# Fused cross-attention and mixture-of-experts kernel: every engine's calls in the attention loop put in another order

## The reference

```python
x = x + xattn(layernorm(x), c, c, Wq, bq, Wk, bk, Wv, bv, Wo, bo, alpha)
x = x + ffn(layernorm(x), Wr, W1, b1, W2, b2)
# xattn, per block of 128 tokens: 16 heads of 16; scores = alpha * 4 * (q.k) / (|q| + |k|)**2 ; softmax over the 128 keys ; @ v ; @ Wo + bo
# ffn: logits = x @ Wr, softmax, top 2 of 8 experts, weights normalised ;
#      out = sum over the 2 experts of weight * (gelu(x @ W1[e] + b1[e]) @ W2[e] + b2[e]),  W1 256 x 1024, W2 1024 x 256
```

## Time and profile before

| | before |
|---|---|
| median of 3 runs | 882.54 us |
| the profiled execution, its own time | 875.53 us |
| its span, first to last instruction | 872.7 us |
| mean granted TensorE clock | 0.985 |
| TensorE busy | 815.5 us (93%) |
| VectorE, ScalarE, GpSimd busy | 644.1, 585.9, 481.2 us |
| the attention loop, first `factors(0)` to the last one's pass | 34 to 458 us |
| the 71 slots | from about 458 us on |

### The profile page before, as it was taken

How to read it: one execution, slowest core, us unless ns; L and a number is a source line. 1 busy time by engine, 2 the same in 40 slices (tenths; PEclk the granted TensorE clock), 3 DMA queues, 4 the chain that set the end, 5 groups by cost and what they waited for, 6 DMA issues and landing times. The chain is left out here.

```text
span 872.7 us, 28779 instructions
## 1 busy us (share of the span) xinstructions
PE 815.5 (93%) x9479; PEld 697.5 (80%) x9479; DVE 644.1 (74%) x2593; ACT 585.9 (67%) x1206; POOL 481.2 (55%) x604
## 2 busy tenths in 40 slices
PE   3899999999999999999888999999999999999995
PEld 2667777777767777777667999999999999999984
DVE  6558688988888888889877788666666666666554
ACT  1488988889888889888866655555555555555542
POOL 5347676879878799887766235422222222222322
PEclk9799999999999999999989999999999999999998
DMA  4212332233322445432459845433333233333221
GB/s 144 81 33 74 98 98 76 83 112 99 123 88 82 162 142 177 135 118 94 148 171 333 280 72 113 97 50 52 50 49 51 50 52 51 51 52 51 39 29 22
DMA packets 61887, 84.69 MB, mean 97 GB/s; under 512 B 9872, under 2 KB 55312, under 8 KB 59568
## 3 DMA queue, kind: packets, MB, share of 16 engines
q1 hardware_dynamic: 47504, 64.26, 23.1%
q0 software_dynamic: 13296, 18.00, 12.3%
q10 hardware_dynamic: 944, 0.60, 0.2%
HBM read 49.86 MB, written 31.92 MB: 94 GB/s over the span
## 5 line engine op out<-in xcount | busy, mean ns | idle before, releaser
L1721 POOL DMA_INDIRECT out<-yw,rb x71 | 111.3, 1567 | 259.0 <-DVE yw L1498 228.1
L1627 POOL TENSOR_TENSOR tw<-tw,tm 128x512 f32<-128x512 f32 x128 | 161.9, 1279 | 43.7 <-DVE tm L1207 43.3
L997 ACT ACTIVATE h<-s_ps,b1t,inv 128x128 f32<-128x128 f32 x288 | 105.0, 467 | 91.3 <-PE s_ps L746 91.2
L997 ACT ACTIVATE h<-u_ps,b1t,inv 128x128 f32<-128x128 f32 x280 | 102.2, 467 | 91.1 <-PE u_ps L746 91.1
L1477 DVE TENSOR_SCALAR hs<-h,hsc 128x512 f16<-128x512 f32 (+1 forms) x146 | 71.0, 486 | 105.7 <-ACT h L997 102.6
L1207 DVE CUSTOM_DVE_ANT_0 tw<-th,s_ps 128x128 f32<-128x128 f32 x512 | 111.7, 282 | 39.1 <-PE s_ps L546 19.0
L1479 DVE SCALAR_TENSOR_TENSOR hs<-h,hsc,hs 128x512 f16<-128x512 f32 (+1 forms) x146 | 107.7, 738 | 5.2
L746 PE MATMUL s_ps<-xt,w1s 128*128 128x128 f16 x1728 | 102.9, 219 | 0.5 <-DVE xt L1464 0.5
L746 PE MATMUL u_ps<-xt,w1s 128*128 128x128 f16 x1680 | 101.8, 221 | 1.1 <-DVE xt L1464 0.6
L770 PE MATMUL pv_ps<-w2s_sb,hs 128*128 x864 | 100.7, 273 | 0.1
L746 PEld LDWEIGHTS s_ps<-xt,w1s 128*128 x1728 | 98.2, 98 | 0.9 <-DVE xt L1464 0.8
(11 more groups left out here) (261 smaller groups left out, 1456.9 us busy)
## 6 DMA issues: line engine op xcount, KB each, us to landing
wl<-L_ffn_W SPq DMA_DIRECT2D x16, 1024.0 KB, 5.3
rb<-xrec SPq DMA_DIRECT2D x71, 132.5 KB, 2.1
w2s<-wst SPq DMA_DIRECT2D x8, 1024.0 KB, 4.6
w2s_sb<-w2s SPq DMA_DIRECT2D x8, 1024.0 KB, 7.3
xin<-x SPq DMA_DIRECT2D x32, 128.0 KB
cin<-ctx SPq DMA_DIRECT2D x32, 128.0 KB, 3.4
xres<-x SPq DMA_DIRECT2D x32, 128.0 KB, 2.3
out<-x SPq DMA_DIRECT2D x30, 128.0 KB, 1.7
```

What stands on the lines that cost most here:

```text
L997: ins = act.activation(h32[n % HBANKS][:, m % width, :], hbank[n % HBANKS][:, o:o + SLOT], ACT.Gelu, scale=inv1[:, bass.ds(ex, 1)].bitcast ...
L1627: pool.tensor_tensor(tw[h][:, i, :, :], tw[h][:, i, :, :], tm[h][:, 4 * i:4 * i + 4].unsqueeze(2).to_broadcast([P, 4, P]), ALU.subtract).t ...
L1721: pool.indirect_dma_start(out[:, :], bass.IndirectOffsetOnAxis(ap=rb[j][:, D + NE:D + NE + 1], axis=0), yw[s % 2][:, :], None, compute_op= ...
```

## The change

No instruction is added or taken out. All five engines' calls in the loop stand in another order, and many with another pair offset, so that a "pass" of the code begins at another place; the banks of the turns are dealt out anew (`TURNS`). SyncE's `store_pads` goes from its end to its front. In the last pair's turns `oc1` gets bank 2 and `wo1` bank 0; VectorE's `residual(0, NP - 1)` goes ahead of `hidden_scales`; ScalarE's `weight_high(NP - 1)` goes into the last pass, ahead of `record_high(0)`. The calls themselves are not edited. In the diff below the indentation is cut by 12, and for TensorE, ScalarE and GpSimd, and the first half of VectorE's, only the new order is shown (the old one stands in the kernel above); "..." marks where old lines are left out.

```diff
@@ -61,18 +61,18 @@
 TURNS = [
-    ("oc0", -5, "ote", 0, 2), ("ex30", -5, "ex30", None, 1), ("rank", -7, "rpos", None, 0), ("ex31", -5, "ex31", None, 2),
-    ("kv1", -3, "qke1", None, 1), ("q1", -3, "qke1", None, 0), ("kv0", -3, "qke0", None, 2), ("q0", -3, "qke0", None, 1),
-    ("ex00", -4, "ex00", None, 1), ("ob1", -5, "on", 1, 2), ("wo0", -5, "x10", None, 0), ("oc1", -5, "ote", 1, 2),
-    ("ex01", -4, "ex01", None, 2), ("ex10", -4, "ex10", None, 1), ("wgr", -4, "wdg", None, 0), ("qk_t0", -3, "kte0", None, 2),
-    ("wo1", -5, "x11", None, 1), ("qk_t1", -3, "kte1", None, 0), ("ex11", -4, "ex11", None, 2), ("rows_t", -3, "rowq", None, 1),
-    ("xct1", -2, "xce1", None, 2), ("xct0", -2, "xce0", None, 0), ("ex20", -4, "ex20", None, 1), ("ex21", -4, "ex21", None, 0),
-    ("ob0", -4, "on", 0, 2), ("wsum", -4, "wcl", None, 1),
+    ("xct0", -3, "xce0", None, 1), ("qk_t0", -4, "kte0", None, 2), ("wo1", -6, "x11", None, 0), ("ex11", -5, "ex11", None, 2),
+    ("qk_t1", -4, "kte1", None, 1), ("rows_t", -4, "rowq", None, 0), ("ex20", -5, "ex20", None, 2), ("wsum", -5, "wcl", None, 1),
+    ("ex21", -5, "ex21", None, 0), ("xct1", -3, "xce1", None, 1), ("ob0", -5, "on", 0, 2), ("ex30", -5, "ex30", None, 0),
+    ("ex31", -5, "ex31", None, 1), ("rank", -7, "rpos", None, 0), ("oc0", -5, "ote", 0, 2), ("kv1", -3, "qke1", None, 1),
+    ("q1", -3, "qke1", None, 0), ("kv0", -3, "qke0", None, 2), ("q0", -3, "qke0", None, 1), ("wo0", -5, "x10", None, 0),
+    ("ex00", -4, "ex00", None, 1), ("ob1", -5, "on", 1, 2), ("ex01", -4, "ex01", None, 0), ("ex10", -4, "ex10", None, 1),
+    ("oc1", -5, "ote", 1, 2), ("wgr", -4, "wdg", None, 0),
 ]
-LATE_BANK = {"wo0": 0, "ob1": 2, "oc1": 0, "wo1": 2, "rank": 0}
+LATE_BANK = {"wo0": 0, "ob1": 2, "oc1": 2, "wo1": 0, "rank": 0}
 def groups(s):
@@ -112,7 +112,7 @@
-             for it in range(2, NP + 5) for what, d, freed, b, bank in TURNS
+             for it in range(3, NP + 5) for what, d, freed, b, bank in TURNS
@@ -356,27 +356,26 @@
     for i in range(b == 0, NSPLIT):
         sp.dma_start(uk[i * STRIP:(i + 1) * STRIP, b, :], uk[0:STRIP, 0, :]).then_inc(sig("set_uk"), 16)
-for it in range(1, NP + 3):
-    if it == 18:
+for it in range(-4, NP + 6):
+    if 0 <= it - 6 < NP:
+        residual(1, it - 6)
+    if NE <= it - 6 < NP - 1:
+        store_w2(it - 6)
+    if it == -4:
         store_pads()
-    if 0 <= it - 2 < NP:
-        load_weights(it - 2)
-    if 0 <= it - 3 < NP - 1:
-        store_x1(0, it - 3)
-    if 0 <= it - 4 < NP - 1:
-        store_x1(1, it - 4)
-    if 0 <= it - 2 < NP:
-        residual(0, it - 2)
-    if NE <= it - 3 < NP - 1:
-        store_w2(it - 3)
-    if 2 <= it + 1 < NP:
-        load(0, it + 1)
-    if 0 <= it - 1 < NP:
-        flat_rows(it - 1)
-    if 0 <= it - 2 < NP:
-        residual(1, it - 2)
-    if 2 <= it + 1 < NP:
-        load(1, it + 1)
+    if 2 <= it - 2 < NP:
+        load(0, it - 2)
+    if 0 <= it - 4 < NP:
+        flat_rows(it - 4)
+        load_weights(it - 4)
+    if 0 <= it - 5 < NP - 1:
+        store_x1(0, it - 5)
+    if 0 <= it - 6 < NP - 1:
+        store_x1(1, it - 6)
+    if 2 <= it - 1 < NP:
+        load(1, it - 1)
+    if 0 <= it - 4 < NP:
+        residual(0, it - 4)
 def load_records(s):
     j = s % U
@@ -627,24 +626,50 @@
     pe.matmul(g[:, 0:1], ones_f[:, :], wss[:, :], start=True, stop=True).then_inc(sig("wsum"), 1)
 router_mean()
...
+for it in range(3, NP + 5):
+    if 0 <= it - 3 < NP:
+        norm(0, it - 3)
+    if 0 <= it - 4 < NP:
+        stack(0, it - 4)
+    if 0 <= it - 5 < NP:
+        factors(3, it - 5)
+    if 0 <= it - 6 < NP - 1:
+        project_out(1, it - 6)
+    if 0 <= it - 5 < NP:
+        scores(3, it - 5)
+        turned(1, 1, it - 5)
+    if 0 <= it - 4 < NP:
+        stack(1, it - 4)
+        rows(it - 4)
+    if 0 <= it - 5 < NP:
+        values(0, it - 5)
+        values(1, it - 5)
+    if it == 4:
+        fold_router()
+    if 0 <= it - 5 < NP:
+        turned(2, 0, it - 5)
+        weight_sum(it - 5)
+        turned(2, 1, it - 5)
+    if 0 <= it - 3 < NP:
+        norm(1, it - 3)
+    if 0 <= it - 5 < NP:
+        heads_back(0, it - 5)
+        turned(3, 0, it - 5)
+        turned(3, 1, it - 5)
+    if 0 <= it - 4 < NP:
+        factors(0, it - 4)
+        scores(0, it - 4)
     if 0 <= it - 5 < NP:
         values(2, it - 5)
...
+        values(3, it - 5)
     if 0 <= it - 7 < NP - 1 and it % 2 == 0:
         ranks(it - 7)
     if 0 <= it - 5 < NP:
...
+        turn_on(0, it - 5)
+    if 0 <= it - 3 < NP:
+        project(1, it - 3)
     if it == 4:
         fold_bias()
...
     if 0 <= it - 4 < NP:
         factors(1, it - 4)
     if 0 <= it - 3 < NP:
@@ -652,42 +677,20 @@
     if 0 <= it - 4 < NP:
         scores(1, it - 4)
         factors(2, it - 4)
+    if 0 <= it - 5 < NP - 1:
+        project_out(0, it - 5)
+    if 0 <= it - 4 < NP:
         turned(0, 0, it - 4)
     if 0 <= it - 5 < NP - 1:
         heads_back(1, it - 5)
...
+    if 0 <= it - 4 < NP:
+        turned(0, 1, it - 4)
+        scores(2, it - 4)
+        turned(1, 0, it - 4)
+    if 0 <= it - 5 < NP - 1:
         turn_on(1, it - 5)
     if 0 <= it - 4 < NP:
...
         weight_products(it - 4)
...
 W1_BYTES = 2 * 2 * DC * H
 W2_BYTES = 2 * 2 * HC * D
@@ -923,62 +926,62 @@
     act.activation(pt[1][:, :, :].rearrange("p i k -> p (i k)")[:, 0:3 * D], s_ps[:, :, :].rearrange("p i k -> p (i k)")[:, 0:3 * D],
                    ACT.Copy).then_inc(sig("set_woc"), 1)
...
+for it in range(3, NP + 5):
+    if 0 <= it - 5 < NP:
+        factors(2, it - 5)
+        turned(0, 0, it - 5)
+        turned(0, 1, it - 5)
+        turned(1, 0, it - 5)
+    if 0 <= it - 6 < NP - 1:
+        o_turned(1, it - 6)
+    if 0 <= it - 4 < NP:
+        roots(it - 4)
     if 0 <= it - 3 < NP:
...
+        x_turned(0, it - 3)
+    if 0 <= it - 4 < NP:
+        stack(0, it - 4)
+    if 0 <= it - 5 < NP:
+        factors(3, it - 5)
+        turned(1, 1, it - 5)
+    if 0 <= it - 4 < NP:
+        stack(1, it - 4)
+    if 0 <= it - 5 < NP:
+        heads_out(0, it - 5)
+        turned(2, 0, it - 5)
+        turned(2, 1, it - 5)
+    if it == 4:
         router_out()
     if 0 <= it - 3 < NP:
...
+        x_turned(1, it - 3)
+    if 0 <= it - 5 < NP:
+        turned(3, 0, it - 5)
+        turned(3, 1, it - 5)
+    if 0 <= it - 4 < NP:
+        factors(0, it - 4)
+    if 0 <= it - 5 < NP - 1:
+        weight_high(it - 5)
+    if 0 <= it - 5 < NP:
+        o_turned(0, it - 5)
+    if 0 <= it - 6 < NP - 1:
+        record_high(1, it - 6)
+    if 0 <= it - 5 < NP:
+        heads_out(1, it - 5)
+    if 0 <= it - 6 < NP - 1 and it % 2:
+        route_exp(it - 6)
     if 0 <= it - 3 < NP:
...
+        v_out(1, it - 3)
+        squares(1, it - 3)
+    if 0 <= it - 4 < NP:
+        factors(1, it - 4)
+    if 0 <= it - 3 < NP:
+        v_out(0, it - 3)
+    if it == NP + 4:
+        weight_high(NP - 1)
+    if 0 <= it - 6 < NP - 1:
+        record_high(0, it - 6)
+    if 0 <= it - 3 < NP:
+        squares(0, it - 3)
 act.activation(gelu_one[:, :], mhalf[:, :], ACT.Gelu)
@@ -1395,21 +1398,24 @@
 for it in range(2, NP + 5):
     if 0 <= it - 6 < NP - 1:
         weight_low(it - 6)
+    if it == SOON_PAIR + 9:
+        soon_rows()
     if 0 <= it - 4 < NP:
         squares(1, it - 4)
...
+    if it == SOON_PAIR + 8:
+        soon_tiles()
     if 0 <= it - 5 < NP:
         scores(1, it - 5)
     if 0 <= it - 6 < NP - 1:
+        residual(0, it - 6)
         heads_back(1, it - 6)
...
     if 0 <= it - 4 < NP:
         squares(0, it - 4)
...
     if 0 <= it - 5 < NP:
         scores(2, it - 5)
+    if it == SOON_PAIR + 8:
+        soon_taken()
+    if 0 <= it - 5 < NP:
         weight_diagonal(it - 5)
     if 0 <= it - 4 < NP:
         norms(it - 4)
@@ -1419,30 +1425,29 @@
         rows(it - 4)
     if 0 <= it - 5 < NP:
         scores(3, it - 5)
+        weight_exponent(it - 5)
+    if 0 <= it - 2 < NP:
+        means(0, it - 2)
+    if 0 <= it - 7 < NP - 1 and it % 2 == 0:
+        counts(it - 7)
+    if 0 <= it - 2 < NP:
+        means(1, it - 2)
+    if 0 <= it - 5 < NP:
         heads_back(0, it - 5)
-        weight_exponent(it - 5)
     if 0 <= it - 7 < NP - 1 and it % 2 == 0:
         shares(it - 7)
+    if it == 4:
+        router_folded()
     if it == SOON_PAIR + 8:
-        soon_rows()
+        soon_slots()
     if 0 <= it - 7 < NP - 1 and it % 2 == 0:
         positions(it - 7)
-    if 0 <= it - 2 < NP:
-        means(0, it - 2)
     if 0 <= it - 6 < NP - 1 and it % 2:
         choose(it - 6)
-    if it == SOON_PAIR + 7:
-        soon_tiles()
-    if it == 4:
-        router_folded()
-    if it == SOON_PAIR + 7:
-        soon_taken()
+    if 0 <= it - 4 < NP:
+        scores(0, it - 4)
     if it == 4:
         router_bias()
-    if 0 <= it - 6 < NP - 1 and it % 2:
-        counts(it - 6)
-    if 0 <= it - 4 < NP:
-        scores(0, it - 4)
 def last_tiles():
@@ -1511,9 +1516,9 @@
```

(37 more changed lines are left out.)

133 lines of the change are left out of this document (4 added, 129 removed).

## The result

| | before | after |
|---|---|---|
| median | 882.29 us (6 runs, 880.40 to 883.78) | 900.67 us (6 runs, 892.86 to 906.06) |
| ratio | | 1.0228, 95% interval 1.0191 to 1.0265 |
| the profiled execution, its own time | 875.53 us | 892.86 us |
| its span | 872.7 us | 890.4 us |
| mean granted TensorE clock | 0.985 | 0.967 |

The account below looks back on a forecast made before the run. The prediction took a pass as bound by a ring, `factors(0)` to `kbr` and back over the flat DMAs. Loop -2.2, start -1.0 and hand-over -0.5 made -3.7 us: 878.8 as a median, range 871 to 890.

Parts of the forecast that it names:

- leg B: From `kbr` over the six flat DMAs to the next `factors(0)`: unchanged, 0; bounds -0.2 and +0.3 us a pass.
- the ring: One loop pass seen as two legs, leg A then leg B, with a mean of 26.52 us a pass before.
- the hand-over: After the loop, last `kbr` to the first `second_product(0)`: -0.5 us, bounds -3 and +3.
- leg A: From `factors(0)` to `kbr`: 20.93 us instead of 21.04; whole gain put at 0.15 a pass, -2.2 over 15 passes.
- the start: First pass, up to `kbr`: -1.0 us, bounds 0 and -1.8.
- This chain now decides: In leg A, VectorE's chain from `scores(1)` sets `kbr` at 20.93 us; TensorE's path would allow it at 20.85.
- Other engines: Moved calls and new banks outside the two legs' chains: 0; bank 0 of `turned(0, 1)` 0 here, bound +0.3 us.
- Rival 1: VectorE's chain has lost its slack and pays for GpSimd maxima beside `norms`: slower, 890 us; chance 0.27.

Follow-up runs that it names:

- e1: Changed kernel plus 16 small filler matmuls on TensorE ahead of the wait for the flat DMAs in `factors(0)`, all passes but the first: 890.19 us, ratio 1.0103.
- e5: Kernel before the change plus a seventh flat DMA of the same size, which TensorE and VectorE also wait for: 913.83 us against 889.37.
- e11: Kernel before the change plus a seventh flat DMA and 12 filler matmuls ahead of the wait for the flat DMAs: 897.92 us, ratio 1.0135.
- e3: Changed kernel with two GpSimd scatters moved: `scatter(3, 1)` back behind `scatter(3, 0)`, `scatter(1, 1)` right ahead of `scatter(2, 0)`: 888.21 us, ratio 1.0010.
- e12: Changed kernel with `soon_rows` alone moved, from the front of VectorE's last pass to behind `soon_slots` one pass earlier: 894.97 us, ratio 1.0162.
- e4: Changed kernel with the one-time steps of the start back in the order of the kernel before: 897.94 us, ratio 1.0196.
- e10: Changed kernel with three flat DMAs of 8 KB, `soon_tiles` and `soon_taken` one pass earlier, `scatter(3, 1)` back beside `scatter(3, 0)`: 869.89 us, ratio 0.9792.
- e9: Changed kernel with `soon_tiles` and `soon_taken` moved from VectorE's last pass to ahead of `scores(0)` one pass earlier: 902.16 us, ratio 1.0152.

## Why the prediction was wrong

**The step that failed** is the sentence in leg B: "Behind `rows` TensorE has 1.01 + 3 us of work against 5.2 to 5.7 of leg B, so its waits there ... cost nothing." The arithmetic was right, and so was the ring: TensorE gets to `factors(0)` early, and a wait there delays nothing. But the stall was 0.56 us in most passes before; the shorter TensorE path ahead of `rows` and the late `values(2)` made it 1.05 at best and 2.67 at worst. The prediction asked only what the stall delays, not what it does to the speed of the next work. It named the clock for the hand-over alone, and so had no rival for it in the loop. e1 (filler: 11 us back) and e5 with e11 (the same clock loss made and undone in the old order) show it. It is not all of the 18 us: in the profiles the clock accounts for 8.2 us in four legs A; the rest lies in the legs B, in the last leg A, in the start and in the hand-over, as below.

**Leg A.** Right in TensorE's path, which got shorter by more than forecast: `rows` at 20.23 to 20.27 instead of 20.4. Wrong in "This chain now decides", said of VectorE's, with `kbr` at 20.93: `scores(1)` began at 10.42 to 10.47 instead of 10.62, and in nine of the 14 legs VectorE idled 0.19 to 0.42 us ahead of `kbr` until `rows` was done. TensorE's arrival decided, as before, and `kbr` came at 20.65 to 20.70. Timeline of VectorE, changed kernel:

```profile
193.11 0.17 DVE L1236 TENSOR_TENSOR r_l<-gen,la 128x8 f32<-128x8 f32 x1 [1.25 <-DMA xres<-x]
...
304.22 0.29 DVE L1192 COPY kbr<-gen 96x256 bf16<-96x256 bf16 x1 [0.22 <-PE gen L471]
```

Sum of its 14 legs: -5.5 for the shorter path; +8.2 from four passes at half clock (22.21, 23.88, 22.46 and 22.24 less 20.65 each); +2.8 in the last; +0.9 in the one of 21.53, whose `rows` waited for `x11`, and VectorE for the load of `residual(1)` (193.11), which the prediction had as covered; +0.2 where it was 20.70; and the kernel before had 1.4 of disturbances of its own: +5.2.

**Leg B.** "Unchanged: 0; bounds -0.2 and +0.3." Measured +0.37 a pass, above the bound, and 4.5 of the 5.2 us in four passes. The bound named scatters beside it, but not their company, packets of the code queues. A leg of e3 (191.90) has 34 packets of a scatter in it and none of code, and took 5.20. Legs with 16 KB or more of code were 5.2 to 6.05 us before, and 5.55 to 6.55 in e3. That the code packets cause it was not tried: no edit moves them by themselves. What was shown is that leg B's length matters twice, by itself and through the clock.

**Other engines.** "The `soon_*` steps move by up to a pass; they are wanted at 455 only: 0." It asked when their results are wanted, and not what they stand ahead of: two of them now precede `scores(1)` and `residual(0)` in VectorE's queue. Their work is 1.8 and 2.9 us there. And bank 0 for `turned(0, 1)`, "freed when TensorE gets there", holds in a full pass; in the last one `soon_rows` holds up `residual(0)`, and the wait was 3.36 us, ten times the bound of 0.3. Without `soon_rows` it was gone (e12).

**Start.** -1.0 forecast, +2.3 measured. 1.1 of it stands at `factors(0)`, whose time varied by 2.2 us between profiles with one and the same order of the start (see e4), so no cause is shown for it. The rest goes with the clock of one leg (0.82 against 0.92), whose length varied by 5 us from profile to profile.

**Hand-over.** The 2.91 went as forecast. The scatter was put at 25.2 us after the last `kbr`; it came at 30.5, at 27.0 without `soon_rows` (e12), and at 21.0 in its old place (e3). TensorE waited 2.57 us for the records, not 6.

**Rival 1** gave the right side and a time of 890, for another reason. `norms` was held up less than before (2.2 to 3.1 us from its first step to its last, against 2.2 to 3.6). Its mechanism shows in another step: the cast of 128x8 at 426.74 took 1.00 us beside a GpSimd maximum that had begun at 426.68, and 0.16 in e10, where none ran. Timelines of GpSimd in the changed kernel and of VectorE in e10_best:

```profile
426.68 1.04 POOL L1632 TENSOR_TENSOR tw<-tw,tm 128x512 f32<-128x512 f32 x1
...
396.58 0.16 DVE L1351 CAST tiles_i<-cnt_f 128x8 int32<-128x8 f32 x1
```

The Trainium skill (SBUF — State Buffer, Who interferes with whom) counts casts among the instructions that can take the ports shared with GpSimd; by that rule the cast waited for the maximum's end, and the trace agrees (427.74 and 427.72).

Another rule would have asked the right question. The Trainium skill (TensorE: Matmul & The Clock Gate, HAM oscillation — how this bites in real kernels) says that waits for a DMA between groups of matmuls let the array's clock be throttled, so that the next group starts cold. The traces agree in kind: 37 of 60 stalls over 1.4 us had 1.2 GHz behind them. By the letter of the section's rule of thumb, though, none of the stalls counted here would have mattered; the measurement decides.

## What to carry to other kernels

A stall of TensorE that delays nothing can still cost: ask how long it is after a change, not only whether something else hides it, and count the passes in which the clock is low behind it. When work moves off the critical leg of a ring, shorten the other leg too (here half as many DMAs of twice the size), or fill the gap. A one-time step is judged by what is queued behind it in its own engine, in the pass with the least cover.

## What the runs showed of the hardware

- 16 matmuls of 128 columns (1.06 us) ahead of a wait, whose result nobody reads, made the kernel 11 us faster; behind the stalls of the trace the clock stayed at 2.4 GHz in 13 of 14 passes, against 10 of 14 without them.
- SyncE issued six flat DMAs of 4 KB in 3.67 us and three of 8 KB in 1.78: some 0.6 us each, whatever their size here. TensorE began 1.2 us after the last issue had ended (legs B of 5.19 us).
- The stalls in e9 and e10 stay unexplained. In e10 VectorE's wait of 2.27 us, ScalarE's of 2.11 and TensorE's of 1.64 end together at 411.1 to 411.5 us, with a code packet of 0.02 MB in the two us before, beside a 1 MB store that took the DMA engines to 94%. e9 has seven such stalls of 1.6 to 2.3 us ahead of `weight_diagonal`; the DMA engines were busy for 81% or more of the 2.3 us up to the end of each, but only in one did a code packet start in that time, and ahead of two there was none in 9 us. So code loading alone doesn't account for them.
